# Mixture-of-experts dispatch on one core: side data scattered, token rows gathered by index

## What is computed

```python
logits = xt @ gate_w
top_p, top_i = lax.top_k(jax.nn.softmax(logits, axis=-1), K)        # E = 8, K = 2, cap = 160
for k in range(K):
    pos = ...                                # rank of the token among those with the same e
    keep = pos < cap
    buf = jnp.zeros((E, cap, D)).at[e, pos_c].set(xt * keep[:, None], mode='drop')
    h = gelu(jnp.einsum('ecd,edf->ecf', buf, w1) + b1[:, None, :])
    y = jnp.einsum('ecf,efd->ecd', h, w2) + b2[:, None, :] + low_rank(buf)
    out = out + y[e, pos_c] * keep[:, None] * w[:, None]
out = out + 0.2 * shared(xt)
```

## Time and profile before

| | |
|---|---|
| median of three runs | 211.71 us (208.94 to 211.88) |
| the profiled execution | 210.92 us, span 209.1 us |
| TensorE busy | 190.2 us (91%), mean granted clock 0.965 |
| VectorE, ScalarE, GpSimd busy | 135.0, 133.9, 110.3 us |
| DMA packets | 27897, 33.03 MB |
| DRAM written | 8.79 MB |

### The profile page before, as it was taken

One profiled execution on the slowest core, in us unless ns is written; L12 is line 12 of the kernel. 1 busy time (PEld: TensorE's weight loads), 2 busy tenths in 40 slices (PEclk: granted clock), 3 DMA queues, 4 the chain that ended last, 5 costly groups with the idle time before them and its releaser, 6 DMA issues.

```text
span 209.1 us, 3942 instructions
## 1 busy us (share of the span) xinstructions
PE 190.2 (91%) x1390; PEld 182.3 (87%) x1390; DVE 135.0 (65%) x294; ACT 133.9 (64%) x285; POOL 110.3 (53%) x162
## 2 busy tenths in 40 slices
PE   6669999999999499999999999999999999999900
PEld 6667777998789499999999999999999999999900
DVE  4547489744762105695879869869869968967020
ACT  2246799913890107968949949949949859778100
POOL 4401404078773006001794895885876867945662
PEclk9978999999999889999999999999999999999975
DMA  5599971522222895018867867866786787601423
GB/s 164 173 296 336 226 249 48 175 72 85 95 92 72 232 327 196 3 13 287 220 114 231 218 158 210 206 201 194 165 234 199 132 263 223 79 0 9 53 31 39
DMA packets 27897, 33.03 MB, mean 158 GB/s; under 512 B 4554, under 2 KB 24772, under 8 KB 27876
## 3 DMA queue, kind: packets, MB, share of 16 engines
q1 hardware_dynamic: 23748, 27.31, 42.7%
q0 software_dynamic: 3760, 4.89, 14.3%
q10 hardware_dynamic: 368, 0.56, 1.0%
HBM read 23.96 MB, written 8.79 MB: 157 GB/s over the span
## 4 chain that ended last, share of the span: by engine, by line
PE 73%; issue 6%; POOL 6%; DMA 6%; DVE 3%; POOLq 1%; ACT 1%; SPq 1%; DVEq 0%
PE hid_ps L791 10%; PE hid_ps L793 10%; PE hid_ps L792 10%; PE y_ps L791 9%; PE y_ps L793 9%; PE y_ps L792 9%; POOL slot_rows L418 5%; PE turn_ps L935 3%; DMA gate_raw<-in_L_ffn_gate_w 3%; DMA slot_rows<-token_row,slot_i 2%; PE row_ps L951 2%; DMA slot_in<-slot_rows 1%; PE hid_ps L812 1%; POOLq L51 1%; PE turn_ps L812 1%
## 5 line engine op out<-in xcount | busy, mean ns | idle before, releaser
L396 POOL DMA_INDIRECT out_rows<-y_row,slot_tok x24 | 44.8, 1866 | 15.8 <-DVE y_row L735 10.9
L618 DVE TENSOR_TENSOR hid_l<-gelu_f,hid_h 128x320 fp32r<-128x320 f32 (+1 forms) x80 | 41.8, 539 | 12.8 <-ACT hid_h L522 11.1
L791 PE MATMUL hid_ps<-xs_h,w_h 128*128 128x288 f32 x128 | 38.2, 298 | 0.0
L793 PE MATMUL hid_ps<-xs_h,w_l 128*128 128x288 f32 x128 | 37.6, 294 | 0.0
L793 PE MATMUL y_ps<-hid_h,w_l 128*128 128x288 f32 x128 | 37.6, 294 | 0.0
L792 PE MATMUL y_ps<-hid_l,w_h 128*128 128x288 f32 x128 | 37.6, 294 | 0.0
L791 PE MATMUL y_ps<-hid_h,w_h 128*128 128x288 f32 x128 | 37.6, 294 | 0.0
L792 PE MATMUL hid_ps<-xs_l,w_h 128*128 128x288 f32 x128 | 37.6, 294 | 0.0
L521 ACT ACTIVATE gelu_f<-hid_ps,bias_now 128x320 f32<-128x320 f32 x64 | 35.2, 549 | 0.9 <-PE hid_ps L793 0.4
L522 ACT ACTIVATE hid_h<-hid_ps,bias_now 128x320 fp32r<-128x320 f32 x64 | 35.5, 555 | 0.0
L594 DVE TENSOR_TENSOR w_l<-w_raw,w_h 128x512 fp32r<-128x512 f32 x36 | 26.4, 752 | 12.5 <-POOL w_h L364 11.8
(11 more groups left out here) (170 smaller groups left out, 413.9 us busy)
## 6 DMA issues: line engine op xcount, KB each, us to landing
w_raw<-in_L_ffn_w SPq DMA_DIRECT2D x16, 1024.0 KB
slot_rows<-empty_row SPq DMA_DIRECT2D x1, 2600.0 KB, 17.1
slot_in<-slot_rows SPq DMA_DIRECT2D x8, 260.0 KB, 3.7
x_in<-in_x SPq DMA_DIRECT2D x2, 512.0 KB, 4.6
w_raw<-in_L_ffn_sw SPq DMA_DIRECT2D x1, 1024.0 KB
out_rows<-base SPq DMA_DIRECT2D x2, 512.0 KB, 3.8
wu_raw<-in_L_ffn_wu SPq DMA_DIRECT2D x24, 32.0 KB
slot_in<-slot_rows SPq DMA_DIRECT2D x8, 65.0 KB, 3.7
```

Of the source, the lines that this page charges most:

```text
L396: pool.indirect_dma_start(out=out, out_offset=bass.IndirectOffsetOnAxis(ap=slot_tok[par][0:n, s:s + 1].bitcast(U32), axis=0), in_=y_row[0: ...
L618: dve.tensor_tensor(hid_l[:, j - 1, 0:n], gelu_f[:, j % 3, 0:n], hid_h[:, j - 1, 0:n].bitcast(F32), ALU.subtract).then_inc(hid_split, 1)
L791: pe.matmul(out_ap, l_h, r_h, start=start, stop=False)
L793: return pe.matmul(out_ap, l_l, r_h, start=False, stop=stop)
```

## The change

`slot_rows` no longer holds slots. Its first 1024 rows of 256 floats hold the token rows in token order, written by two plain DMAs on SP, each when half of them are copied out of PSUM. The other DRAM scratch, `cond_rows`, now holds four floats for each of 3072 slots (384 per expert, laid out by partition): weight and token number. It is filled with empty entries (48 KB), and the sixteen scatters write 16 bytes per row into it. The slot numbers change with this layout, so `place_tokens` has other steps. Once the scatters have landed, SP loads all sides by one DMA, VectorE makes from them row numbers for reading and for writing (`side_data`, four operations, for all experts at once), and GpSimd gathers each expert's rows by index with three indirect DMAs (`gather`), for experts 0 and 1 then, for later ones in its `period`. `load_slots`, the large fill, the second copy of the rows and the `side_data` of each expert are gone. Counting comes after hidden tile 4 and no longer 6, placing after split 5 and no longer 8, and `turn_slots(0, 0)` behind output block 2 and no longer 1.

```diff
-W_COL, ID_COL = D, D + 1
+SIDE = 4
+ROW = D + SIDE
+W_COL, ID_COL = 0, 1
 ST = (SLOTS + P - 1) // P
 ST_ROWS = [min(P, SLOTS - s * P) for s in range(ST)]
+PER_P = E * ST
+NEXT_TILE = float(P * PER_P - 1)
...
+        tile_of = sb("tile_of", [P, 2, NT, K])
+        token_side = sb("token_side", [P, NT, K, SIDE])
+        no_token = sb("no_token", [P, PER_P, SIDE])
+        slot_side = sb("slot_side", [P, E, ST, SIDE])
+        slot_free = sb("slot_free", [P, E, ST])
+        slot_row = sb("slot_row", [P, E, ST])
+        slot_tok = sb("slot_tok", [P, E, ST], I32)
+        slot_src = sb("slot_src", [P, E, ST], I32)
...
-        token_row = [sb(f"token_row{k}", [P, NT, ROW]) for k in range(K)]
+        token_row = sb("token_row", [P, NT, D])
...
-        slots_a = slot_rows.rearrange("(e s) f -> e s f", e=E)[:, 0:2 * P, :].rearrange("e (t p) f -> e p t f", p=P)
-        slots_b = slot_rows.rearrange("(e s) f -> e s f", e=E)[:, 2 * P:SLOTS, :]
...
+        x_rows = slot_rows.rearrange("a b -> (a b)")[0:T * D].rearrange("(t f) -> t f", f=D)
+        x_rows_v = x_rows.rearrange("(t p) f -> p t f", p=P)
+        sides = cond_rows.rearrange("a b -> (a b)")[0:P * PER_P * SIDE].rearrange("(s f) -> s f", f=SIDE)
+        sides_v = sides.rearrange("(p s) f -> p s f", p=P)
...
-            def load_slots(e, par, first=False):
-                if not first:
-                    sp.wait_ge(slots_turned, (e - 1) * KD)
-                    sp.wait_ge(slots_sided, (e - 1) * KD)
-                sp.dma_start(slot_in[par][:, 0:2, :], slots_a[e]).then_inc(slots_in[par], 16)
-                sp.dma_start(slot_in[par][0:ST_ROWS[2], 2, :], slots_b[e]).then_inc(slots_in[par], 16)
...
-            sp.wait_ge(empty_made, 2)
-            sp.dma_start(fill_v, empty_row[:, :].unsqueeze(1).to_broadcast([P, E * SLOTS // P, ROW])).then_inc(filled, 16)
-            sp.dma_start(spare_v, empty_row[0:64, 0:D].unsqueeze(1).to_broadcast([64, SLOTS // 64, D])).then_inc(spare_out, 16)
+            sp.wait_ge(empty_made, 3)
+            sp.dma_start(sides_v, no_token[:, :, :]).then_inc(filled, 16)
...
+            for h in range(2):
+                sp.wait_ge(rows_copied, (h + 1) * NT // 4)
+                half = slice(h * HTILES, (h + 1) * HTILES)
+                sp.dma_start(x_rows_v[:, half, :], token_row[:, half, :]).then_inc(x_rows_out[h], 16)
...
-            sp.wait_ge(consts, 11)
-            load_slots(0, 0, first=True)
-            load_slots(1, 1, first=True)
+            sp.dma_start(slot_side[:, :, :, :].rearrange("p e s f -> p (e s) f"), sides_v).then_inc(side_in, 16)
...
                 load_first(e + 1)
-                load_slots(e, e % 2)
                 load_second(e + 1)
...
-            def side_data(e, par):
-                pool.wait_ge(slots_in[par], (e + (2 - par)) * 16)
-                pool.tensor_copy(slot_w[par][:, :], slot_in[par][:, :, W_COL]).then_inc(slot_math, 1)
-                pool.tensor_scalar(slot_free[:, :], slot_in[par][:, :, ID_COL], float(T), None,
-                                   ALU.is_ge).then_inc(slot_math, 1)
-                pool.wait_ge(slot_math, e * SIDE + 2)
-                pool.tensor_tensor(slot_spare[:, :], slot_free[:, :], slot_local[:, :], ALU.mult).then_inc(slot_math, 1)
-                pool.wait_ge(slot_math, e * SIDE + 3)
-                pool.tensor_tensor(slot_row[:, :], slot_spare[:, :], slot_in[par][:, :, ID_COL],
-                                   ALU.add).then_inc(slot_math, 1)
-                pool.wait_ge(slot_math, e * SIDE + 4)
-                pool.tensor_copy(slot_tok[par][:, :], slot_row[:, :]).then_inc(slots_sided, KD)
+            def gather(e, par):
+                if e >= 2:
+                    pool.wait_ge(slots_turned, (e - 1) * KD)
+                for s in range(ST):
+                    n = ST_ROWS[s]
+                    pool.indirect_dma_start(
+                        out=slot_in[par][0:n, s, :], out_offset=None, in_=x_rows,
+                        in_offset=bass.IndirectOffsetOnAxis(ap=slot_src[0:n, e, s:s + 1].bitcast(U32),
+                                                            axis=0)).then_inc(slots_in[par], 16)
...
-            for b in range(NT // 2):
-                pool.wait_ge(rows_copied, b + 1)
-                pool.tensor_copy(token_row[1][:, 2 * b:2 * b + 2, 0:D],
-                                 token_row[0][:, 2 * b:2 * b + 2, 0:D]).then_inc(rows_twice, 1)
...
-                        out=slot_rows, out_offset=bass.IndirectOffsetOnAxis(ap=slot_i[:, t, k:k + 1].bitcast(U32), axis=0),
-                        in_=token_row[k][:, t, :], in_offset=None, bounds_check=E * SLOTS - 1,
+                        out=sides, out_offset=bass.IndirectOffsetOnAxis(ap=slot_i[:, t, k:k + 1].bitcast(U32), axis=0),
+                        in_=token_side[:, t, k, :], in_offset=None, bounds_check=P * PER_P - 1,
                         oob_is_err=False).then_inc(dispatched, 16)
+            pool.wait_ge(slots_sided, 1)
+            for h in range(2):
+                pool.wait_ge(x_rows_out[h], 16)
+            gather(0, 0)
+            gather(1, 1)
...
                     combine(e - 1, 1 - par)
-                side_data(e, par)
+                if e + 2 < E:
+                    gather(e + 2, par)
...
-                step(dve.tensor_tensor(base_of[:, :, 1], base_of[:, :, 1], best[:, :], ALU.add))
...
-                step(dve.tensor_tensor(base_of[:, :, :], base_of[:, :, :], pos[:, :, :], ALU.add))
                 dve.wait_ge(slots_known, 1)
+                step(dve.tensor_tensor(pos[:, :, 1], pos[:, :, 1], best[:, :], ALU.add))
+                step(dve.scalar_tensor_tensor(out=base_of[:, :, :], in0=pos[:, :, :], scalar=float(PER_P),
+                                              in1=base_of[:, :, :], op0=ALU.mult, op1=ALU.add))
+                for s in range(1, ST):
+                    step(dve.tensor_scalar(tile_of[:, s - 1, :, :], pos[:, :, :], float(s * P), -NEXT_TILE, ALU.is_ge,
+                                           ALU.mult))
+                    step(dve.tensor_tensor(base_of[:, :, :], base_of[:, :, :], tile_of[:, s - 1, :, :], ALU.add))
                 dve.tensor_tensor(slot_i[:, :, :], base_of[:, :, :], slot_f[:, :, :], ALU.add).then_inc(slots_known, 2)
...
+            def side_data():
+                dve.wait_ge(side_in, 16)
+                token = slot_side[:, :, :, ID_COL]
+                dve.tensor_scalar(slot_src[:, :, :], token, float(T - 1), None, ALU.min)
+                dve.tensor_scalar(slot_free[:, :, :], token, float(T), None, ALU.is_ge).then_inc(side_math, 1)
+                dve.wait_ge(side_math, 1)
+                dve.tensor_tensor(slot_row[:, :, :], slot_free[:, :, :], slot_local[:, :, :], ALU.mult).then_inc(side_math, 1)
+                dve.wait_ge(side_math, 2)
+                dve.tensor_tensor(slot_tok[:, :, :], slot_row[:, :, :], token, ALU.add).then_inc(slots_sided, 1)
...
-            place_tokens()
+                if j == 5:
+                    place_tokens()
...
+                    side_data()
+                if t == HTILES + 2:
                     slots_lo_part(0)
...
-                pe.wait_ge(slots_in[par], (e + (2 - par)) * 16)
+                pe.wait_ge(slots_in[par], (e // 2 + 1) * 16 * ST)
...
-                    if h == 0 and j == HT - 3:
+                    if h == 0 and j == HT - 5:
...
-                    if h == 1 and t == 1:
+                    if h == 1 and t == 2:
```

52 lines of the change are left out of this document (22 added, 30 removed).

## The result

| | before | changed |
|---|---|---|
| median | 211.05 us (208.94 to 211.88) | 237.19 us (236.82 to 238.22) |
| profiled execution | 210.92 us, span 209.1 | 237.00 us, span 235.2 |
| TensorE busy | 190.2 us (91%) | 193.9 us (82%) |
| DRAM written | 8.79 MB | 5.13 MB |

The ratio is 1.129, 95% interval 1.122 to 1.136: slower, as forecast, but 11 us above the 226 us forecast and outside its range of 216 to 232.

The account below looks back on a forecast made before the run. TensorE was taken to bound the experts' stage, with one 3.05 us hole at the dispatch and little room on GpSimd. 210.92 + 4.3 (dispatch, including 1.6 for slot numbers) + 11.0 (periods) = 226 us, range 216 to 232.

Parts of the forecast that it names:

- Fill removed: Dropping the large fill and its 2.6 MB of writes: nothing waited for it, 0 us.
- Slot numbers earlier: Counting and placing earlier delays VectorE's splits, so TensorE stalls in the first shared output block until 41.2: +1.6 us.
- Scatters "whatever their size": Dispatch: GpSimd issues the sixteen one by one, about 40 to 65.7, winning 2.3 us; small rows landing sooner change nothing.
- The chain behind them: After the scatters: side load, VectorE's four operations, three gathers; TensorE goes on at 78.0, not 70.69: +4.3 us net.
- The landing term of 3.74: Dispatch: from the third gather's start at 74.3 to its rows' landing, 3.74 us, the last scatter's time.
- Wanted later: 0: Dispatch: the second expert's gathers and the weight loads starting at about 66 are wanted later, so cost 0 us.
- The period: Experts' periods 1 to 5: three gathers between combine and bias delay the bias 2.3 us each, less 0.5 once: +11.0 us.
- Rival 1: Periods: gathers slip in between VectorE's operations, bias 1.1 us late, +9.3 in all, 220 us; chance 0.19.
- rival 2: Periods and dispatch: gathers cost what combining scatters cost, +22, 233 us; chance 0.10.
- rival 3: Periods: gathers fit between combine and bias, no late bias, only the dispatch is lost, 215 us; chance 0.10.
- rival 4: Stalls bring TensorE's clock to 1.2 GHz; a second stretch at the dispatch costs 1.7 us, 228 us; no separate chance.
- something unseen: Any outcome outside the listed cases, no place or size given; chance 0.04.

Follow-up runs that it names:

- bias first: Changed kernel with each period's three gathers issued last, behind the bias copy and the second-weight casts: 215.8 us (1.026).
- one input instead of two: Changed kernel with VectorE's subtractions of two SBUF tiles replaced by operations with one SBUF input, for the weights of experts 1 to 7: 223.3 us.
- with the bias on time: Changed kernel with only the bias copy put ahead of the three gathers, the second-weight casts staying behind them: 224.6 us (1.065).
- the kernel with 14 more: Kernel before with fourteen small gathers of 32 rows of 128 bytes added on GpSimd where it is idle: 217.5 us (1.035).
- the late placing: Changed kernel with counting and placing back where the kernel before has them: 229.2 us (1.090), 228.7 us in a repeat.
- the best version: Changed kernel, gathers behind bias and casts, `side_data()` before shared row 4, next weight loads held until the first expert's gathers land: 209.25 us (0.993), 209.4 us (0.995).
- the 27 memsets added: The best version with 27 tiny memsets added on GpSimd in its idle time at 9 to 17 us: 209.4 us (1.000).

## Why the prediction was right or wrong

On the chips without the hole the changed kernel takes 226.9 and 228.3 us, near the sum of 226; on the others, where it was first measured, 237.2 and 238.6 us, 11 to 13 us above it. The step that failed is the one on the scatters: it took TensorE, VectorE and ScalarE beside them to run on as before (0 us), and a hole of 9.4 us stood there. The marks of the profiled executions, as more than before; the first gelu of all starts at 27.15 before:

| part | forecast | 226.9 us | 228.3 us | first measurement |
|---|---|---|---|---|
| start to the first gelu of all | 0 | -1.5 | 1.3 | 0.05 |
| from there to the first expert's first gelu | 4.3 | 3.3 | 4.0 | 13.3 |
| from there to the last expert's | 11.0 | 11.9 | 10.5 | 10.65 |
| from there to the end | 0 | 2.1 | 2.1 | 2.1 |

That 226.9 us lies so near is luck in part: an early start of 1.5 us, which is no part of the change, and 1.0 us too much taken for the dispatch nearly make up for the 2.1 us at the end that were missing and 0.9 us in the periods.

- **Fill removed, 0 us.** Nothing waited for the fill before, and DRAM writes fell by 3.7 MB with no time won. It was not tried alone.
- **Slot numbers earlier, +1.6 us.** The last slot number starts at 38.85 (said: 38.8), TensorE stalls 1.26 us at 39.95, and shared row 1 comes at 44.80, 1.7 us later than before (43.07). Right.
- **Scatters "whatever their size".** Right for their issue: with 16-byte rows in the kernel before it is 211.0 us, and with the bias first the sixteen take 21.5 us from the first start to the last, as before (21.6). The last starts at 61.51 and lands at 63.6, not 65.7, since the small rows land in 2.1 us and not in 3.74. As was said, that changes nothing: the sides then land at about 65.4, and VectorE comes to them behind shared row 5 at 69.5.
- **The chain behind them.** With no hole (bias first): shared row 5 at 69.19, first gather 70.52, third 73.10, TensorE 76.94; said 69.3, 71.5, 74.3 and 78.0. From the slot rows' end to the first gather it took 0.3 us and not 1.0. A gather of 128 rows takes 1.00 to 0.97 and one of 64 0.93, below the 1.08 taken. The landing term of 3.74 came out (3.84) by chance: it is 2.7 to 3.0 us with the DMA engines quiet and 6.8 to 7.4 with the weight loads in its way, and here the third gather starts when most of them have passed (DMA share 1.08 from 70 to 73, 0.64 from 73 to 76). "Wanted later: 0" for those loads was the wrong step. The Trainium skill's price (DMA: Bandwidth & Descriptors, Anatomy of one DMA — SWDGE (gpsimd) path), 2.15 us as an estimate, is 0.5 us below the shortest measured, 2.7. TensorE stood 4.8 to 4.9 us before the transposes (said: 5.8), and the clock behind it cost 1.6 us in the kernel of 226.9 us and 2.7 us in that of 228.3 us (said: 1.7).
- **The period, +11.0 us.** Between the first gelus of experts 1 and 6 it was 86.83 us and not 75.42: +11.4. The wait of the first gather (it ends 0.90 us behind VectorE's run, said 0.87) and the delay of the bias (2.24 us, said 2.3) are as forecast, and one input instead of two takes the first away. Rival 1 ("no lock" among the chances: the gathers don't wait for VectorE) fell by the first gather's 2.0 to 2.48 us, rival 2 by the others' 0.91 to 0.98, rival 3 by the late bias, and rival 4 in the periods: the granted clock is 1.00 from 94 to 208 us, though TensorE stands about 1.8 us in each period. (The bound of 3.4 us a period comes to 3.6 by its own terms; nothing hangs on it.) One sentence of this step was wrong: the casts don't merely move along, with the bias on time they alone still cost most of it (7.8 of 10.5 us). And the period behind the last gathers, taken as unchanged, gives 0.75 us back (14.27 us).
- **The end, +1.9 us.** Not in the sum at all: the step "out of GpSimd's part go five small operations; in come three gathers" counted the gathers' issue and not what 24 more of them leave to the end. Shown by the kernel with 14 more.
- **The hole, 9.4 us and its clock, 9 to 10 us in all** (13.3 us in the second row of the table against 3.3 and 4.0). This is the step that failed: "If small rows land sooner it changes nothing" looked only at when they land, not at the engines beside them, and the case "something unseen" got 0.04. What brings the late signals is not settled. Shown: they depend on the chip; the last of them comes 1.8 to 3.4 us behind the last scatter or gather of the row; the changed dispatch has them with 16 and with 512 bytes a row, the old one with 1 KB rows doesn't on the same chips (by its time on both, and by the trace of the kernel with more gathers on one); small gathers bring them too. Not tried on such a chip: the late placing, rows of 1 KB in the changed kernel, and the best version.

## What to carry to other kernels

A load moved from the sync queue to GpSimd costs where it stands in GpSimd's list: put it behind everything another engine waits for, the casts as well as the bias, which gave back 11 to 12.5 us here. Then look at what shares the DMA engines with it: holding the next expert's weight loads back until the first gathers had landed was worth 6.5 us. The whole redesign, done well, comes to 0.7% on one chip, 0.5% on another and nothing on a third (there with the 27 memsets added); and a kernel measured on one chip only may carry 10 us that another chip doesn't show.

## What the runs showed that was not expected

- On two of six chips, and in the first measurement, TensorE's signals came 2.5 to 11 us late while GpSimd issued indirect DMAs (the changed dispatch, or 128-byte gathers), and its clock fell to 0.50 in the hole that follows; on the other four never.
- Each indirect DMA of GpSimd adds about 0.08 us between the last one's issue and the end of the program.
- The landing of a gather of 64 rows takes 2.7 us on quiet DMA engines and up to 7.4 us with 1 MB weight loads in flight.
- The 128x8 bias copy takes 2.42 us where it is the first of GpSimd's operations beside VectorE's two-input run (109.55 above; the run lasts to 111.92), and 0.20 behind the gathers: the wait falls to whatever GpSimd does next, and a gather behind the copy takes 1.04.
